# First stage of a four-layer graph network: scores earlier in the step, mask added by VectorE, output projection two steps behind

## The reference, cut to what matters

```
h = relu(layernorm(x))
q, k, v = heads(h @ Wq.T + bq), heads(h @ Wk.T + bk), heads(h @ Wv.T + bv)   # 8 heads of 32
scores = einsum('bhqd,bhkd->bhqk', q, k) / sqrt(32)
scores = where(adj == 0, -inf, scores)
out = einsum('bhqk,bhkd->bhqd', softmax(scores), v)
x = x + merge(out) @ Wo.T + bo
```

## Time and profile before

| what | value |
|---|---|
| median of 3 runs | 1662.28 us (1660.25 to 1665.63) |
| profiled execution, its own time | 1662.14 us |
| its span | 1660.3 us |
| busy in the span: PE / DVE / ACT / POOL | 1471.5 / 1283.4 / 1021.6 / 440.7 us |
| granted clock of TensorE, mean | 0.965 |

### The profile page before, as it was taken

The page is one execution under the profiler, slowest core; times in us unless marked ns, Lnnn a source line. Parts: engine busy times, 40 slices in busy tenths (PEclk is TensorE's granted clock), DMA queues, the critical chain, the costliest instruction groups (busy, mean ns, idle before and its releaser), DMA issues.

```text
span 1660.3 us, 36159 instructions
## 1 busy us (share of the span) xinstructions
PE 1471.5 (89%) x11454; PEld 1242.8 (75%) x11517; DVE 1283.4 (77%) x3002; ACT 1021.6 (62%) x3208; POOL 440.7 (27%) x745
## 2 busy tenths in 40 slices
PE   5789999999879977999999999999999999975776
PEld 4678888888779965787877777787877778764554
DVE  4877777777567758788888888888888888754997
ACT  3568788788645546565666556565666656533776
POOL 1112212212046642031222223132222222122332
PEclk9899999999979988999999999999999999996999
DMA  7400000000000000000000000000000000000112
GB/s 235 133 2 0 0 0 0 0 0 0 1 1 0 0 0 1 1 1 1 0 0 0 0 0 0 0 0 0 0 0 0 0 0 1 1 1 7 64 63 70
DMA packets 23873, 24.22 MB, mean 15 GB/s; under 512 B 1936, under 2 KB 23184, under 8 KB 23696
## 3 DMA queue, kind: packets, MB, share of 16 engines
q1 hardware_dynamic: 23824, 23.60, 4.5%
HBM read 15.21 MB, written 8.39 MB: 14 GB/s over the span
## 4 chain that ended last, share of the span: by engine, by line
PE 42%; DVE 26%; ACT 18%; issue 11%; POOL 1%; DVEq 0%; DMA 0%; ACTq 0%; SPq 0%; POOLq 0%
ACT probs L894 9%; PE bank L1323 4%; PE bank L1436 4%; PE bank L1160 3%; DVE headsT_lo L695 3%; PE bank L1374 3%; DVE probs L706 3%; PE bank L1246 2%; DVE em L688 2%; PE bank L1389 2%; PE bank L1237 2%; ACT probs L1005 2%; PE bank L1278 2%; PE bank L1290 2%; PE bank L1291 2%
## 5 line engine op out<-in xcount | busy, mean ns | idle before, releaser
L894 ACT ACTIVATE probs<-bank,negtop 128x128 f32<-128x128 f32 x512 | 185.8, 415 | 47.6 <-DVE negtop L628 47.5
L273 POOL TENSOR_TENSOR var_eps<-mv,eps_tile 128x2 f32<-128x2 f32 x128 | 38.3, 299 | 636.6 <-DVE mv L261 636.6
L1330 PE MATMUL bank<-aggT_hi,wh_hi 128*128 128x256 f32 x512 | 148.5, 290 | 12.2 <-DVE em L690 9.2
L289 ACT ACTIVATE h<-x_all,shift,rstd 128x256 f32 (+1 forms) x256 | 139.9, 596 | 31.5 <-POOL shift L279 31.5
L1343 PE MATMUL bank<-wout_hi,headsT_hi 128*128 128x258 f32 x512 | 156.2, 305 | 0.0
L980 ACT CAST aggT_hi<-bank 128x512 fp32r<-128x512 f32 x128 | 75.2, 588 | 120.3 <-PE bank L1323 120.3
L1330 PE MATMUL bank<-aggT_lo,wh_hi 128*128 128x256 f32 x512 | 145.1, 283 | 0.0
L1330 PE MATMUL bank<-aggT_hi,wh_lo 128*128 128x256 f32 x512 | 145.1, 283 | 0.0
L1343 PE MATMUL bank<-wout_lo,headsT_hi 128*128 128x258 f32 x512 | 144.5, 282 | 0.0
L1343 PE MATMUL bank<-wout_hi,headsT_lo 128*128 128x258 f32 x512 | 144.2, 282 | 0.0
L1323 PE MATMUL bank<-probsT,h 128*128 128x512 f32 x256 | 133.2, 625 | 0.5 <-ACT probsT L1013 0.5
(11 more groups left out here) (209 smaller groups left out, 4718.2 us busy)
## 6 DMA issues: line engine op xcount, KB each, us to landing
x_all<-in_x SPq DMA_DIRECT2D x32, 256.0 KB, 2.8
out_x<-x_all SPq DMA_DIRECT2D x32, 256.0 KB, 2.1
wh<-in_L_gnn_W_heads SPq DMA_DIRECT2D x2, 512.0 KB, 7.7
a_heads<-in_L_gnn_a_heads SPq DMA_DIRECT2D x1, 1024.0 KB, 11.0
wout<-in_L_gnn_W_out SPq DMA_DIRECT2D x1, 1024.0 KB, 11.1
raw<-in_L_gnn_W SPq DMA_DIRECT2D x1, 512.0 KB, 5.6
ffn<-in_L_gnn_w SPq DMA_DIRECT2D x2, 256.0 KB, 7.1
consts<-in_shape_consts SPq DMA_DIRECT2D x1, 322.0 KB, 2.7
```

Source lines behind the costliest of these rows:

```text
L289: last = nc.scalar.activation(h[:, p, c, :], x_all[:, bass.ds(g * G + c, 1), :].rearrange("p a d -> p (a d)"), ACT.Relu, bias=shift[:, p, ...
L894: last = nc.scalar.activation(probs[:, r, i, :], bank[4 + r][:, i * N:(i + 1) * N], ACT.Exp, bias=negtop0[:, r, i:i + 1], scale=float(DH) ...
L1330: last = nc.tensor.matmul(bank[3 + i % 2][:, o * G * N:(o + 1) * G * N], w[:, k, i, o * N:(o + 1) * N], src[:, k, i].rearrange("p c n -> p ...
```

## The change

Only the first stage and its setup are changed.

- Order on TensorE: q projection; first half of the k projection; output projection of group t-2; second half of k; transposes 0, 1, 2 of group t-1 (banks 2, 3, 1); scores of group t; v; transposes of h; transposes 3 (bank 2); transposes of the row sums; attention times v of group t-1.
- The four mask products are gone; the scores start their banks themselves. VectorE adds hide0 (bf16) to the scores while it copies them from the bank to probs in SBUF (`masked`), the maxima are taken from probs, and the exponentials work in place in probs. The banks are free as soon as they are copied.
- The factor 1/sqrt(32) is applied where q is copied (and to its bias in setup), so the four small scalings and the scale of the exponentials go.
- att0T is split in a high and a low part by VectorE (a copy and a subtraction), Wo likewise in setup, and the output projection is three fp32r products, 12 in all, in bank 2, in the step after.
- ScalarE: exponential 3 of group t-1, then in the same step 0, 1 and 2 of group t.

```diff
@@ VectorE, setup
+            nc.vector.tensor_scalar(bq_c[:, :], bq_c[:, :], float(DH) ** -0.5, None, ALU.mult)
+            nc.vector.tensor_copy(woT_hi[:, :, :], bank[3][:, :].rearrange("p (c o) -> p c o", c=2)).then_inc(weights_dve, 1)
+            dve.wait_ge(weights_dve, 6)
+            nc.vector.tensor_tensor(woT_lo[:, :, :], bank[3][:, :].rearrange("p (c o) -> p c o", c=2), woT_hi[:, :, :].bitcast(FP32),
+                                    ALU.subtract).then_inc(weights_dve, 1)
@@ VectorE, step0
+                def top(r):
+                    dve.wait_ge(masked0, g * 4 + r + 1)
+                    nc.vector.tensor_reduce(negtop0[:, r, :], probs[:, r], AX.X, ALU.max, negate=True).then_inc(top0_step, 1)
+
+                def masked(r):
+                    if positive(g):
+                        dve.wait_ge(pT0_full, g * 4 - 3 + r)
+                    dve.wait_ge(s0_full, g * 4 + r + 1)
+                    nc.vector.tensor_tensor(probs[:, r], bank[4 + r][:, :].rearrange("p (k n) -> p k n", k=4),
+                                            hide0[:, :, :], ALU.add).then_inc(masked0, 1)
+
+                if z:
+                    dve.wait_ge(o_full, gz + 1)
+                    dve.wait_ge(pre[0].bias, gz + 1)
+                    nc.vector.tensor_tensor(x_group(gz), bank[2][:, :].rearrange("p (c d) -> p c d", c=G), x_group(gz),
+                                            ALU.add).then_inc(pre[0].x, 1)
...
+                if f:
+                    if positive(g):
+                        dve.wait_ge(p0_ready, g * 4)
+                    masked(0)
+                    masked(1)
+                    top(0)
+                    masked(2)
+                    top(1)
+                if b:
                     probs_T(3)
                 n, gn, _ = at.group(-1)
+                if f:
+                    masked(3)
                 if n:
                     dve.wait_ge(hT0_hi, gn + 1)
...
+                if f:
+                    top(2)
                 if b:
...
+                    dve.wait_ge(aT_ready, gb * 3 + 1)
                     if positive(gb):
                         dve.wait_ge(o_full, gb)
...
+                    nc.vector.tensor_copy(att0T_hi[:, :, :, :], att0T[:, :, :, :]).then_inc(aT_ready, 1)
+                    dve.wait_ge(aT_ready, gb * 3 + 2)
+                    nc.vector.tensor_tensor(att0T_lo[:, :, :, :], att0T[:, :, :, :], att0T_hi[:, :, :, :].bitcast(FP32),
+                                            ALU.subtract).then_inc(aT_ready, 1)
+                pre_dve(dve, 0, at)
+                stats_written(dve, 0, at)
+                if f:
+                    top(3)
+                moments_dve(0, at)
@@ TensorE, step0
+                    project_T(bank[0], wkT_hi, wkT_lo, (0,))
+                if z:
+                    pe.wait_ge(aT_ready, gz * 3 + 3)
+                    for c in range(G):
+                        for k in range(KC):
+                            for src, w in ((att0T_hi, woT_hi), (att0T_hi, woT_lo), (att0T_lo, woT_hi)):
...
+                    last.then_inc(o_full, 1)
+                if f:
+                    project_T(bank[0], wkT_hi, wkT_lo, (1,)).then_inc(k_full, 1)
                 if b:
                     probs_T(0)
                     probs_T(1)
-                if f:
+                    probs_T(2)
```

More of the change, by code:

```diff
@@ L183, in build_program @@
                 woT = sb_0("woT", [N, KC, D])
+                woT_hi, woT_lo = [sb_0(f"woT_{part}", [N, KC, D], F32R) for part in ("hi", "lo")]
                 hT_hi = sb_0("hT_hi", [N, KC, G, N], F32R)
@@ L190, in build_program @@
                 att0T = sb_0("att0T", [N, KC, G, N])
+                att0T_hi, att0T_lo = [sb_0(f"att0T_{part}", [N, KC, G, N], F32R) for part in ("hi", "lo")]
             with ExitStack() as layer1:
@@ L617, in step0 @@
                     dve.wait_ge(rT_ready, gb + 1)
+                    nc.vector.tensor_tensor(att0T[:, :, :, :], bank[2][:, :].rearrange("p (k c n) -> p k c n", k=KC, c=G),
+                                            rsumT[:, :, :, :], ALU.mult).then_inc(aT_ready, 1)
+                    dve.wait_ge(aT_ready, gb * 3 + 1)
                     if positive(gb):
                         dve.wait_ge(o_full, gb)
[L620 to L628, removed]
-                if f:
[L631 to L639, removed]
+                    nc.vector.tensor_copy(att0T_hi[:, :, :, :], att0T[:, :, :, :]).then_inc(aT_ready, 1)
[4 more added lines that the diff above has]
+                stats_written(dve, 0, at)
+                if f:
+                    top(3)
+                moments_dve(0, at)
                 if isinstance(at.t, int) and 0 <= at.t < 4:
@@ L917, in step0 @@
                 if b:
[L918 to L924, removed]
                     act.wait_ge(rT_full, gb + 1)
                     if positive(gb):
-                        act.wait_ge(aT_ready, gb)
+                        act.wait_ge(aT_ready, gb * 3 - 2)
                     nc.scalar.copy(rsumT[:, :, :, :], bank[3][:, :].rearrange("p (k c n) -> p k c n", k=KC, c=G)).then_inc(rT_ready, 1)
-                ahead, ga, _ = at.group(-2)
-                if ahead and positive(ga - 1):
-                    act.wait_ge(hT0_full, ga - 1)
-                pre_act(act, 0, at, -2)
                 if f:
-                    exp(0, g, p)
                     exp(1, g, p)
+                    exp(2, g, p)
             act.wait_ge(pool_setup, 1)
@@ L1166, in step0, with project_T @@
                 b, gb, pb = at.group(1)
-                def project_T(dst, w_hi, w_lo):
-                    for o in range(KC):
+                z, gz, _ = at.group(2)
+                def project_T(dst, w_hi, w_lo, parts=(0, 1)):
+                    for o in parts:
                         for k in range(KC):
@@ L1186, in probs_T, with scores @@
                     if positive(gb) and r == 0:
-                        pe.wait_ge(aT_ready, gb)
+                        pe.wait_ge(pre[0].x, gb)
                     if positive(gb) and r == 1:
-                        pe.wait_ge(pre[0].x, gb)
-                    if r == 2:
+                        pe.wait_ge(rT_ready, gb)
+                    if r == 2 and f:
+                        pe.wait_ge(q_ready, g + 1)
+                    if r == 3:
                         pe.wait_ge(pT0_act, gb * 2 + 1)
-                    if r == 3:
-                        pe.wait_ge(pT0_dve, gb * 2 + 1)
                     for k in range(4):
-                        last = nc.tensor.transpose(bank[2 + r % 2][:, k * N:(k + 1) * N], probs[:, r, k, :], ident)
+                        last = nc.tensor.transpose(bank[(2, 3, 1, 2)[r]][:, k * N:(k + 1) * N], probs[:, r, k, :], ident)
                     last.then_inc(pT0_full, 1)
+                def scores(k):
+                    for c in range(G):
+                        for r in range(4):
+                            i = k * G + c
+                            rows = slice(r * DH, (r + 1) * DH)
+                            last = nc.tensor.matmul(bank[4 + r][:, i * N:(i + 1) * N], qT[rows, k, c, :], kT[rows, k, c, :],
+                                                    start=True, stop=True)
+                            if i == KC * G - 1:
+                                last.then_inc(s0_full, 1)
                 if f:
```

81 lines of the change are left out of this document (36 added, 45 removed).

## The result

| | kernel before | changed kernel |
|---|---|---|
| median | 1663.95 us (4 runs) | 1678.17 us (4 runs, 1677.21 to 1679.07) |
| ratio to before | 1 | 1.0088, 95% interval 1.0067 to 1.0109 |
| profiled execution, span | 1660.3 us | 1675.4 us |

The change costs 0.9%, 14 us. The forecast was 1669.1, 7 us more than before, with a range of 1655 to 1681: slower, as said, but by twice as much.

What follows compares the result with a forecast made beforehand. A ring of exponentials, TensorE's queue, scores and first maximum was taken as the bound, with VectorE becoming its engine. First steps +9.5, steady steps 0, end -2.5 gave +7.0 us: 1669.1, range 1655 to 1681.

Steps and rivals of the forecast that it cites:

- the ring: Steady step: projection, x add, transposes, scores, masked copies, att0T parts, next projection; 12.34 us against 12.43, no gain in 26 steps.
- copy 3: VectorE's third probabilities copy, sixth of nine operations ahead of att0T; attention times v waits for it, TensorE idling 0.9 us.
- The cheap mask: Rival: the mask add takes 0.43 us instead of 0.69, first-stage steps fall to 11.4, total 1640; chance 0.15.
- the copy at 0.69: Rival: att0T's high-part copy takes 0.69 us, not 0.43, and row-sum widening is held up; 26 x 0.37 more, 1679; chance 0.17.
- The late weights of step 0: VectorE's preparation of later weights in the first step: starts 8.9 us after kT instead of 7.01, +1.9.
- a collision: Steady steps: 0.1 us allowed for GpSimd's bias add touching VectorE's work, raising the step from 12.34 to 12.43.
- TensorE's 0.9 wait: Steady step, ahead of attention times v: TensorE idles 0.9 us for VectorE's third probabilities copy, but hides it.
- First steps: Setup and steps 0 to 4: 0.9 + 1.9 + 0.8 + 2.4 + 2.4 + 1.1 = +9.5 us, bounds 4 and 14.
- GpSimd among the rivals: Rival: GpSimd's bias add falls on the att0T parts in the steady steps, 26 x 1.1 = 29 us, total 1698; chance 0.05.
- the widening's risk: Steady step: GpSimd's 1.28 us bias add only touches VectorE's widening of the row sums, costing 0.1 us.
- The end: From kT of step 31 to the last x add's end: 22.3 us against 24.85, -2.5, bounds -4 and 0.
- Later stages move as a whole: Stages after the first wait for it and shift together, adding 0 us of their own.

Runs made afterwards that it cites:

- experiment 3: Changed kernel with eight fp32 output projection products of att0T, still two steps behind, without att0T's high and low parts: 1673.87 us, ratio 1.0066.
- experiment 6: Changed kernel with GpSimd's bias adds of the first steps made to wait until VectorE has prepared the later weights: 1678.39 us, ratio 1.0103.
- experiment 2: Changed kernel with the output projection behind the row sums' transposes (bank 4) and its x add behind att0T_lo: 1666.85 us, ratio 1.0027.
- experiment 1: Changed kernel with the output projection writing bank 4 instead of bank 2, so transposes no longer wait for the x add: 1664.29 us, ratio 1.0016.
- 8: Changed kernel with the projection behind the row sums' transposes (bank 4), as eight fp32 products without att0T's parts: 1646.44 us, ratio 0.9908.
- 4: Changed kernel with the mask again written by four TensorE products ahead of the scores, maxima and exponentials reading the banks: 1678.80 us, ratio 1.0093.

## Why the prediction was right and wrong

**Sign and mechanism.** Right that VectorE joins the ring and that TensorE's saved issue turns into waits: 24 us less busy in 300, and the two waits (0.30 for the x add, 0.89 for copy 3, predicted 0.9) are there. Durations held: masked copies 0.68, the high part 0.43, exponentials from SBUF 0.39 apart. The cheap mask did not come, nor the copy at 0.69. The late weights of step 0 began 8.92 after kT (predicted 8.9), those of step 2 13.1 (predicted 14.0, which counted an x add of 0.6 that now stands behind them). The size was not right: 14 us against 7.

**The failed step: "the ring closes at 12.34 against 12.43 ... no gain in 26 steps".** It closed at 12.62, because three terms of the sum were too small by 0.10 to 0.14 each:

| term | predicted | measured |
|---|---|---|
| projection to x add | 1.74 | 1.87 (208.32 to 210.19) |
| x add to transposes | 0.74 | 0.84 (210.19 to 211.03) |
| transposes to scores | 1.29 | 1.43 (211.03 to 212.46) |
| scores to the masked copy | 1.19 | 1.20 (to 213.66) |
| masked copy to att0T_lo | 6.64 | 6.54 (to 220.20) |
| att0T_lo to projection | 0.74 | 0.75 (220.95) |
| sum | 12.34 | 12.63 |

The first term was an addition slip: 11 x 0.12 + 0.1 + 0.42 is 1.84. In the second the 0.05 for handing over had no row behind it; the third was put together from rows of four and of eight transposes. 0.19 a step over my 12.43 is 26 times 0.19 = 4.9 us. The miss of the sum itself is 0.29: the 12.43 held 0.1 for a collision that never came in the steady steps, and so was nearer than the sum by luck. The period is over the 12.3 to 12.5 that I had named, and under the 12.7 from which I would have called it wrong.

**What the ring left out.** I followed one ring, through att0T's parts, and did not see that a second one with nearly the same length runs through copy 3, attention times v and TensorE's queue. I had written that TensorE's 0.9 wait was hidden. It was hidden by 0.12 us only; experiment 3 shows it. So a reader of the prediction would have mended the wrong thing (the parts of att0T), and I did. Nor had I seen that VectorE's hT_lo holds the q projection in this second ring (218.57), 0.09 behind attention times v.

**First steps, +9.5 against +11.1.** By parts: setup +0.7 (0.9 predicted), step 0 +3.0 (1.9), step 1 +1.7 (0.8), step 2 +2.7 (2.4), step 3 +2.4 (2.4), step 4 +0.6 (1.1). The excess of steps 0 to 2, 1.1, 0.9 and 0.3, stands beside one lengthened operation in each, by 1.1, 0.6 and 0.6, and experiment 6 took these away. Without them (2.4 together) it would be +8.7: setup, step 4 and the late weights of step 2 came out smaller than predicted, and hid a part of what was missing. I had GpSimd among the rivals at 0.05 but looked for it in the steady steps, where the changed kernel has none (its widening stays at 0.49); it sat in steps 0 to 2.

In the rows, a two-input product with both inputs in SBUF and the widening end only after the whole bias add (the products 1.09 and 0.54 after it, the widening 0.28). Where the widening was first (209.28 against 209.37 in experiment 2) it kept its 0.49 and the bias add took 1.54; where a product of 1.23 was first (103.16 against 103.38 in the changed kernel) the bias add took 2.13. Operations that read one input from PSUM were not lengthened. That is the rule of the Trainium skill (SBUF — State Buffer, Who interferes with whom), where whoever issues first holds the shared ports for its whole instruction; the same list names a scalar operation of the widening's kind, in its two-port form, beside the two-input ones. Whether the widening runs in that form no run shows. I had read the rule for two-input operations alone and put the widening's risk at 0.1.

**The end, -2.5 against -2.6,** was right. **"Later stages move as a whole"** held but for 1.7 us. The second stage ended 13.1 later than before and the third began 13.1 later (its first transposes, 613.12 and 626.24). The first product of its line 1330 (1356 in the changed kernel) came 15.9 later, the last stage 16.8 later, and the end 15.1 later. In the stretch where the third begins, the granted clock, a mean over both of its levels, was 0.81 against 0.87. The windows 622 to 720 of the changed kernel and 609 to 703 of the kernel before:

```profile
622.00:720.00 98.00, 75.09 (x417) 54.14 (x421) 71.48 (x142) 54.83 (x141) 17.79 (x28) 0.81 0.00 1
```

```profile
609.00:703.00 94.00, 71.05 (x418) 52.59 (x422) 71.34 (x142) 54.81 (x141) 17.62 (x28) 0.87 0.00 1
```

Four products of that stretch, first before and then after the change, show the two levels:

```profile
632.47 1.98 PE L1323 MATMUL bank<-probsT,h 128*128 128x512 f32 x4
...
646.10 3.78 PE L1349 MATMUL bank<-probsT,h 128*128 128x512 f32 x4
```

They started 13.6 later and ended 15.4 later. No experiment was made on why the clock differs there.

**What each part is worth,** as far as the runs separate it (in per cent of 1660 us): the scale in q alone -0.4; the x add between the projection and the transposes +0.7 (experiment 1 against the changed kernel); the parts of att0T where the change has them 0.2, inside both intervals (3), and 1.2 once the projection stands in the gap (8 against 2). In both pairs eight fp32 products replace twelve fp32r ones as well. Where the mask is added made no difference in the changed order (4). That VectorE's masking is what makes the gap usable, because bank 4 is free by then, is argued, not shown.

## What to carry to other kernels

Before you call a wait hidden, write down the ring that would close without it and its length: where two rings are 0.1 us apart, an edit that shortens one alone looks useless (3), one that shortens both pays (1), and the first edit can pay later, where its engine has become the bound (8). Move work into the gap that a new order opens, not in front of the operation that opens it. When VectorE becomes the bound, look for GpSimd beside its SBUF operations and delay GpSimd: one added wait on it, together with a smaller setup, gave 0.9% here.

## What the hardware showed that I had not expected

- The widening, 0.49 by itself, took 1.26 to 1.54 us when GpSimd's add (1.27) had begun 0.3 to 0.04 us before it; two-input products went from 1.23 to 2.34 and from 0.69 to 1.33. What was added, 1.11 and 0.64 us, is 0.14 to 0.15 less than what was left of the bias add when they began (1.25 and 0.79).
- From the start of a 512-element VectorE operation to the TensorE product that waits for it are 0.84 us for the x add (210.19 to 211.03), 0.82 for copy 3 (216.65 to 217.47), but 0.75 for att0T_lo (220.20 to 220.95) and 0.73 for hT_lo (217.84 to 218.57), with records of 0.68 to 0.69. I had taken 0.74 for all; why they differ is open.
- The last stage took 134.3 us in the profiled execution of the changed kernel, 136.3 in that of experiment 6 and 135.9 in that of the kernel before, with the same work. Its cause is open.
